# A planner that orders single engine parts by their own data needs, loads in order of use, row sums apart from values, and a second expert weight pack over early memory

## The chip, the cores and the metric

The kernel runs on one core of one Trainium2 chip. The metric is the device time of one execution in microseconds, as the median of several runs. The core has five engines, each with its own instruction queue worked in order: PE (matrix products and transposes, written into PSUM banks), ACT and DVE (element work; they also empty the banks), POOL (small element work), and SP (issues the DMAs). They meet only at semaphores.

## The reference

Four layers, each a cross-attention and a feed-forward block with a gated residual, on x of 2 sequences x 512 tokens x 128 features, and a context of 2 x 77 tokens:

```
x = x + tanh(g_xattn[0]) * L0_xattn(layernorm(x), ctx, ctx, mask)  # 16 heads of 8, masked
x = x + tanh(g_ffn[0])   * L0_ffn(layernorm(x))                    # 128 -> 512 relu -> 128
x = x + tanh(g_xattn[1]) * L1_xattn(layernorm(x), ctx, ctx)        # one key head for 16 query heads
x = x + tanh(g_ffn[1])   * L1_ffn(layernorm(x))                    # shared silu MLP 352 + 16 experts x 64, top 2
x = x + tanh(g_xattn[2]) * L2_xattn(layernorm(x), ctx, ctx)
x = x + tanh(g_ffn[2])   * L2_ffn(layernorm(x))                    # 32 experts x 32, top 1 by argmax
x = x + tanh(g_xattn[3]) * L3_xattn(layernorm(x), ctx)             # 3 iterations of slot attention with a GRU cell
x = x + tanh(g_ffn[3])   * L3_ffn(layernorm(x))                    # int8 product with one 128 x 128 matrix
```

All experts are computed for all tokens, and the router's weights are multiplied in.

## The kernel before

**Tiling.** A "half" is one sequence: 512 tokens, 4 tiles of 128. Everything of a half (x, xn, q, wide and so on) has its own copy, so that the two halves never wait for each other's data. They share the engines, the 8 PSUM banks and the weights. A third stream, "preparation", makes keys and values of all layers, masks and constants of the slot layer.

**The steps of a half.** A layer normalisation is `norm` (DVE statistics, POOL power -0.5) and `norm_end` (DVE writes xn). `turn` transposes xn (PE, ACT). Attention is `query`, four `maxima` (PE scores, DVE row maxima), `max_rows`, three `scores` (PE, then ACT writes four exponentials to `wide`), three `values`, each of which multiplies the exponentials both with a head mask (`heads_of`, the row sums) and with the values (`v_cols`), then `sum_rows` (transpose, DVE reciprocal), `spread` (PE brings the reciprocals back, DVE multiplies) and `project`. `bias` on POOL adds biases to x meanwhile. Layer 1's feed-forward has `gates1` (router), `shared`, `experts`, `weights_turn`, `weigh`, `down_shared`, `down1`, `back`. Layer 2's has `router`, `choice_turn`, `hidden2`, `choose`, `down2`. The slot layer has, three times, `square`, `slots_turn`, `slot_products`, `slot_scores`, `hidden`, `slot_inverse`, four `gru`, `gru_r`, `gru_z`, `gru_end`.

**What sets the order.** The order on each engine is made when the program is built, by `schedule()`. `stream_steps` writes the steps of each stream as a list; one step is a chain over several engines with a duration for each (`pe=0.86, act=0.5`). A step waits for the one before it in its list, but for those marked `on` (the next may follow once their first part has ended) and `side` (nobody in the list waits). Half 1 may not start before `LAG` = 21.937 us. At every turn the part that can start first is put next; small constants shift this rank: `PREFER_STREAM`, `PREFER_ENGINE`, `PER_STEP_LEFT`, and `LATER`, a table with one hand-set shift in tenths of a microsecond for each step of each stream (some 190, 190 and 14 numbers from -82 to 40). `EARLY` and `OPEN` = 3 place the expert steps relative to each other; `OPEN` is how many `hidden2` banks may be open before the first `choose`. `BankTurn` gives every PE result the bank that is free first. Where the planner sees PE idle, after `FILL_FROM` = 20 us, `keep_warm` puts products of `ident16` with `halves` (bf16, 512 columns) into the gap, whose result nobody reads.

**Loads.** SP issues all loads in one row at the start (L642 to L668): x of half 0, ctx_t, attn0, cols, consts, x of half 1, mask, halves, ctx_4, rows, and the later weights. Pack ffn2 lies over the memory of ffn1; SP waits for the last expert products of both halves (`banks.full("y", 3, b)`, L670) and then loads it (L671).

## Time and profile before

| | us |
|---|---|
| median of 3 runs | 359.32 |
| the three runs | 359.07, 359.32, 362.11 |
| the profiled execution | 361.95 |
| its span, first to last instruction | 360.2 |
| PE busy in the span | 328.1 (91%) |
| DVE busy | 225.3 (63%) |
| ACT busy | 136.9 (38%) |
| POOL busy | 47.8 (13%) |

The profiled execution is 2.6 us above the median, and 1.75 us of it lie outside the span. PE's busy time contains the products that `keep_warm` adds. Busy shares are means over a start, a middle and an end that have different limits, so each is read by itself.

### The profile page before, as it was taken

The numbers are of one execution on the slowest core, as the hardware profiler recorded it, in microseconds if no ns is written. First come the engines' busy times: TensorE is split into PE (matmuls) and PEld (weight loads), VectorE is DVE, ScalarE is ACT, GpSimd is POOL, SyncE is SP. The second block draws the span as 40 slices with busy tenths as digits, with TensorE's granted clock in tenths as the row PEclk, the third lists the DMA queues.
The fourth block names the chain that finished last, engine by engine and source line by source line (L and its number), as shares of the span: only waits on it lengthen the run. The fifth ranks groups of instructions, "written<-read, shape, count | busy, mean of one in ns | idle before, by whom it ended". The sixth has DMA issues, their size and how long they took to land.

```text
span 360.2 us, 5043 instructions
## 1 busy us (share of the span) xinstructions
PE 328.1 (91%) x1843; PEld 175.3 (49%) x1843; DVE 225.3 (63%) x635; ACT 136.9 (38%) x287; POOL 47.8 (13%) x73
## 2 busy tenths in 40 slices
PE   0789989998888899999999997899999999999994
PEld 0455453463424543554444434455445677677442
DVE  2596574366628551677766728345353797798995
ACT  1226326331451565225321361711232366646200
POOL 6113112031010100010200020101021311101110
PEclk9999999998989999999999999999999999999998
DMA  7940000000000000000000300000000000000001
GB/s 195 354 198 0 2 0 2 1 0 3 0 2 0 2 0 0 2 0 1 1 2 0 118 11 0 2 0 2 0 0 0 2 1 2 0 2 0 0 14 47
DMA packets 6669, 8.68 MB, mean 24 GB/s; under 512 B 2907, under 2 KB 5493, under 8 KB 6389
## 3 DMA queue, kind: packets, MB, share of 16 engines
q1 hardware_dynamic: 6645, 8.37, 7.0%
q8 instruction: 15, 0.25, 0.3%
q14 instruction: 9, 0.07, 0.1%
HBM read 7.84 MB, written 0.52 MB: 23 GB/s over the span
## 4 chain that ended last, share of the span: by engine, by line
PE 76%; DVE 15%; ACT 6%; issue 1%; DMA 1%; SPq 0%; DVEq 0%; ACTq 0%
PE psum L754 68%; DVE mx L1443 6%; ACT wide L1124 4%; PE psum L838 3%; DVE wide L1610 1%; PE psum L956 1%; PE psum L874 1%; DMA w_attn<-in_attn 1%; PE psum L1052 1%; PE psum L1079 1%; ACT xn_t L1124 1%; PE psum L791 0%; DVE rinv_d L1452 0%; DVE wide L1575 0%; DVE rinv L1449 0%
## 5 line engine op out<-in xcount | busy, mean ns | idle before, releaser
L754 PE MATMUL psum<-xn_t,w_ffn 128*128 128x512 f32 (+1 forms) x136 | 66.6, 608 | 0.8 <-ACT xn_t L1124 0.8
L754 PE MATMUL psum<-wide,w_ffn 128*128 128x512 f32 (+1 forms) x92 | 47.4, 603 | 0.5 <-DVE wide L1535 0.3
L754 PE MATMUL psum<-halves 128*128 128x512 bf16 x178 | 43.9, 379 | 0.2 <-DVE q_lo L1435 0.2
L1443 DVE TENSOR_REDUCE mx<-psum 128x4 f32<-128x308 f32 x96 | 38.7, 471 | 7.3 <-PE psum L754 7.1
L1124 ACT ACTIVATE wide<-psum 128x512 f32<-128x512 f32 x72 | 36.6, 624 | 11.0 <-PE psum L754 10.8
L1124 ACT ACTIVATE q<-psum 128x512 f32<-128x512 f32 (+1 forms) x40 | 23.5, 594 | 44.1 <-PE psum L754 43.8
L754 PEld LDWEIGHTS psum<-xn_t,w_ffn 128*128 128x128 f32 (+1 forms) x136 | 24.9, 190 | 28.8 <-issue 25.9
L698 POOL TENSOR_SCALAR nw<-mv 128x4 f32<-128x4 f32 x16 | 3.6, 227 | 218.7 <-DVE mv L1309 218.7
L754 PEld LDWEIGHTS psum<-halves 128*128 128x128 bf16 x178 | 17.3, 99 | 17.2 <-issue 1.7
L1315 DVE TENSOR_SCALAR xn<-x,mv,nw 128x128 f32<-128x128 f32 x64 | 17.8, 347 | 10.9 <-POOL nw L699 10.7
L754 PE MATMUL psum<-w_attn,q 128*128 128x128 f32 x192 | 23.7, 276 | 0.2 <-DVE q L1459 0.2
L754 PEld LDWEIGHTS psum<-wide,w_ffn 128*128 128x128 f32 (+1 forms) x92 | 16.3, 192 | 15.0 <-issue 8.5
L754 PEld LDWEIGHTS psum<-w_attn,q 128*128 128x128 f32 x192 | 22.5, 192 | 2.0 <-issue 1.1
L1124 ACT ACTIVATE xn_t<-psum 128x512 f32<-128x512 f32 x18 | 11.1, 615 | 30.5 <-PE psum L838 16.5
L1124 ACT ACTIVATE wide<-psum,cols 128x512 f32<-128x512 f32 x12 | 8.2, 687 | 31.2 <-PE psum L754 31.2
L754 PE MATMUL psum<-wide,heads_of 128*32 128x512 f32 x144 | 20.0, 626 | 0.0
L754 PE MATMUL psum<-wide,v_cols 128*32 128x512 f32 x144 | 19.6, 614 | 0.0
L1528 DVE TENSOR_TENSOR wide<-q,psum 128x512 f32<-128x512 f32 x16 | 11.0, 685 | 11.4 <-PE psum L754 9.8
L754 PE MATMUL psum<-wide 78*128 78x386 f32 x48 | 17.8, 496 | 0.2 <-DVE wide L1598 0.2
L699 POOL TENSOR_TENSOR nw<-nw,minus_half 128x4 f32<-128x4 f32 x16 | 16.6, 1036 | 1.3
L1306 DVE BATCH_NORM_STATS2 stats<-x 128x6 f32<-128x128 f32 x64 | 13.9, 280 | 3.9 <-DMA x<-in_x 3.5
L1435 DVE SCALAR_TENSOR_TENSOR q_lo<-psum,cols,q_hi 128x512 fp32r<-128x512 f32 x6 | 4.5, 751 | 18.5 <-ACT q_hi L1180 18.5
(208 smaller groups left out, 492.5 us busy)
## 6 DMA issues: line engine op xcount, KB each, us to landing
w_ffn<-in_ffn SPq DMA_DIRECT2D x1, 2088.5 KB, 12.6
w_ffn<-in_ffn SPq DMA_DIRECT2D x1, 1104.0 KB, 5.0
w_attn<-in_attn SPq DMA_DIRECT2D x1, 640.0 KB, 8.1
w_attn<-in_attn SPq DMA_DIRECT2D x2, 288.0 KB, 5.8
x<-in_x SPq DMA_DIRECT2D x2, 256.0 KB, 3.1
w_ffn<-in_ffn SPq DMA_DIRECT2D x1, 512.0 KB, 6.7
out<-x SPq DMA_DIRECT2D x2, 256.0 KB, 2.3
rows<-in_rows SPq DMA_DIRECT2D x1, 468.0 KB, 6.0
```

Source lines behind the costliest of these rows:

```text
L699: G.tensor_tensor(nw[:, b, 2, :], nw[:, b, 0, :], minus_half[:, :], ALU.pow)\
L754: return nc.tensor.matmul(out_, lhs, rhs, start=start, stop=stop, **kw)
L838: last = nc.tensor.transpose(bk[:, t * P:(t + 1) * P], (y if stage == 7 else xn)[:, b, t, :], ident)
L874: last = nc.tensor.transpose(bk[:, t * P:(t + 1) * P], mx[:, b, t, :], ident)
L956: last = nc.tensor.transpose(bk[:, t * P:(t + 1) * P], tile[:, b, t * P:(t + 1) * P], ident)
L1052: last = nc.tensor.transpose(bk[:, t * P:(t + 1) * P], slots[:, b, t, :], ident)
L1124: A.activation(dst, banks.bank(*name)[0:rows_, 0:cols_], fn, **kw).then_inc(drained["act"], 1)
L1306: last = V.bn_stats(stats[:, b, t, :], x[:, b, t, :])
L1315: last = V.tensor_scalar(xn[:, b, t, :], x[:, b, t, :], mv[:, b, t, 0:1], nw[:, b, 2, t:t + 1], ALU.subtract, ALU.mult)
L1435: V.scalar_tensor_tensor(q_lo[:, b, :], banks.bank("q", layer, b), col(f"bq{layer}"), q_hi[:, b, :].bitcast(F32), ALU.add, ALU.subtract).t ...
L1443: last = V.tensor_reduce(mx[:, b, t, lane_heads(g)], banks.bank("max", layer, b, t, g)[:, 0:GK].rearrange("p (h k) -> p h k", k=CTX), AX.X ...
L1528: V.tensor_tensor(wide[:, b, c, :], act_s[slot][:, b, :], banks.bank("e_u", b, c), ALU.mult)\
```

## The change

1. `schedule()` is replaced. Every step is split into its parts on single engines, and each part names the parts that it reads from (`after`, `then`). A part can be planned once these are planned. `left` is the length of the longest chain of parts that hang on it. The rank is its earliest time, plus `later`, minus 0.1 x `left`. `LAG`, `PREFER_STREAM`, `PREFER_ENGINE`, `PER_STEP_LEFT`, `EARLY` and `OPEN` go. `LATER` now is one number for each stream: 0 for half 0, 2.1 us for half 1, -0.7 us for the preparation. `LOADED` gives the time at which a part's load is taken to have landed.
2. `values` is split into `sums` (row sums) and `values`; each has its own bank and its own exit on ACT. `shared` and `experts` become 11 pairs of `gate` and `up`; `back` at stage 3 is split, with `back_shared` for the shared MLP; `hidden` of the slot layer becomes three.
3. `spread` uses a transpose instead of a product with the identity.
4. Loads: cols, the identity alone, wq of layer 0 and ctx_t go ahead; x of half 1 goes behind ctx_4. `turn` 0 no longer waits for POOL's constants.
5. ffn2 now lies over the masks, attn0 and ffn0 (tile `early`), and its load waits for `y` of stage 1.
6. Eight products on a zeroed tile run on PE before its first step; one memset on DVE makes the tile.

```diff
-LAG = 21.937
-PREFER_STREAM = 0.0, 0.075, -0.739
-PREFER_ENGINE = {"pe": 0.0, "act": 1.11, "dve": 0.291, "pool": 1.091}
-PER_STEP_LEFT = 0.008
-OPEN = 3
+LEAD = {("pe", "turn"): 0.3}
+LEFT = 0.1
+WARM_UP = 8
+LOADED = {("dve", "norm", 0, 0): 3.4, ("pe", "keys_in", 2, 0): 5.0, ("pe", "turn", 0, 0): 4.2, ("pe", "query", 0, 0): 4.8,
+          ("dve", "mask_parts", 2): 6.5, ("pe", "values_in", 2, 0): 9.5, ("dve", "norm", 1, 0): 10.0,
...
         for j in range(NJ):
-            step("values", layer, j, on=j < NJ - 1, pe=1.72, **({"act": 1.0} if j == NJ - 1 else {}),
-                 after=[(PREPARATION, "values_in", layer), (b, "scores", layer, j)])
-        step("sum_rows", layer, pe=0.44, dve=0.92)
-        step("spread", layer, pe=0.88, dve=0.6)
+            evicted = {"act": 0.5} if j == NJ - 1 else {}
+            for phase, made in (("sums", 0), ("values", layer)):
+                step(phase, layer, j, after=[at("act", "scores", layer, j), prepared("dve", "values_in", made)]
+                     + in_order("pe", phase, layer, j), pe=0.86, **evicted)
+        step("sum_rows", layer, after=[at("act", "sums", layer, NJ - 1)], pe=0.44, dve=0.92)
+        step("spread", layer, after=[at("dve", "sum_rows", layer)], then={"dve": [at("act", "values", layer, NJ - 1)]},
+             pe=0.44, dve=0.6)
...
+        for st in waiting:
+            if all(steps[key].end is not None for key in st.after):
+                at = max([steps[key].end for key in st.after], default=0.0) - LEAD.get(st.key[:2], 0.0)
+                at = max(at, free[st.engine], LOADED.get(st.key, 0.0))
...
+                if st.engine == "pe":
+                    at = max(at, banks.deal(units_of(st.phase, st.half, st.args), drained)[1])
+                if at < float("inf"):
+                    rank = at + st.later - LEFT * st.left
...
             load_x(0)
+            sp.dma_start(cols[:, :], a["cols"]).then_inc(loaded["cols"], 16)
+            sp.dma_start(consts[:, 0:P], a["consts"][:, 0:P]).then_inc(loaded["ident"], 16)
+            sp.dma_start(packs["attn0"][:, 0:wq_n], a["attn0"][:, 0:wq_n]).then_inc(loaded["wq0"], 16)
             sp.dma_start(ctx_t[:, :], a["ctx_t"]).then_inc(loaded["ctx_t"], 16)
...
-                sp.wait_ge(*banks.full("y", 3, b))
+                sp.wait_ge(*banks.full("y", 1, b))
             sp.dma_start(packs["ffn2"][:, :], a["ffn2"]).then_inc(loaded["ffn2"], 16)
...
                 for t in range(T):
-                    last = mm(bk[:, t * P:(t + 1) * P], rinv_d[:, b, t, :], ident)
+                    last = nc.tensor.transpose(bk[:, t * P:(t + 1) * P], rinv_d[:, b, t, :], ident)
...
+            def gate(b, k):
+                r = SHC[k][1] if k < SHARED else P
+                if k >= 2:
+                    act.wait_ge(*banks.emptied("up", b, k - 2))
+                empty(act_s[k % 2][0:r, b, :], ACT.Silu, ("gate", b, k), r)
```

## Rows read from the trace of the kernel before

**Rows 1.** The head of the page: span, and busy time of each engine.
```profile
span 360.2 us, 5043 instructions
PE 328.1 (91%) x1843; PEld 175.3 (49%) x1843; DVE 225.3 (63%) x635; ACT 136.9 (38%) x287; POOL 47.8 (13%) x73
```

**Rows 2.** Busy time of each engine by stretch; first column is the stretch.
```profile
core 0: us, PE busy (x) PEld busy (x) DVE busy (x) ACT busy (x) POOL busy (x), PEclk, DMA share, GB/s
0.00:54.00 54.00, 39.91 (x293) 22.82 (x294) 34.79 (x104) 17.05 (x35) 14.56 (x26) 1.00 0.37 125
54.00:288.00 234.00, 221.87 (x1177) 110.45 (x1174) 130.14 (x383) 89.89 (x173) 25.94 (x35) 0.99 0.02 6
288.00:361.00 73.00, 66.28 (x378) 42.07 (x376) 60.39 (x149) 29.96 (x80) 7.31 (x12) 0.98 0.03 8
```

**Rows 3.** Groups by form, PE, the idle products: whole span, then from 288.
```profile
L754 PE MATMUL psum<-halves 128*128 128x512 bf16 x178 | 43.9, 379 | 0.2 <-DVE q_lo L1435 0.2
...
L754 PE MATMUL psum<-halves 128*128 128x512 bf16 x136 | 31.8, 379 | 0.0
```

**Rows 4.** Chain that ended last, first 50 us: start, length, what.
```profile
5.98 1.28 ACT L1128
...
9.07 1.25 DVE minus_max L1361
...
12.56 2.07 PE psum L754 x2
...
17.04 6.27 DVE mx L1443 x16
```

**Rows 5.** Instructions in order of time (start, length, engine), the first layer normalisation and query.
```profile
5.23 1.04 POOL L699 TENSOR_TENSOR nw<-nw,minus_half 128x4 f32<-128x4 f32 x1
...
10.25 1.10 DVE L1315 TENSOR_SCALAR xn<-x,mv,nw 128x128 f32<-128x128 f32 x4
...
14.68 0.69 ACT L1180 ACTIVATE q_hi<-psum,cols 128x512 fp32r<-128x512 f32 x1 [2.16 <-PE psum L754]
```

**Rows 6.** The page's DMA issues: size, us to landing.
```profile
halves<-in_halves SPq DMA_DIRECT2D x1, 384.0 KB, 5.6
```

**Rows 7.** Groups by form, PE: spread, the transposes of maxima, the row sums.
```profile
L754 PE MATMUL psum<-consts,rinv_d 128*128 128x128 f32 x48 | 6.7, 283 | 2.8 <-DVE mx L1443 2.5 <-DVE rinv_d L1452 0.3
...
L874 PE MATMUL psum<-consts,mx 128*128 128x128 f32 x24 | 3.9, 283 | 0.9 <-DVE mx L1443 0.9
...
L754 PE MATMUL psum<-wide,heads_of 128*32 128x512 f32 x144 | 20.0, 626 | 0.0
```

**Rows 8.** DVE in order of time: half 1's maxima ahead of half 0's spread.
```profile
46.47 3.16 DVE L1443 TENSOR_REDUCE mx<-psum 128x4 f32<-128x308 f32 x8
49.56 0.67 DVE L1459 TENSOR_TENSOR q<-q,psum 128x512 f32<-128x512 f32 x1
```

**Rows 9.** DVE in order of time: the shared MLP's way back into x.
```profile
167.81 1.13 DVE L1542 SCALAR_TENSOR_TENSOR x<-psum,route_s,x 128x128 f32<-128x128 f32 x4 [0.20 <-PE psum L956]
```

**Rows 10.** DVE in order of time: hidden, then the inverse, in the slot layer.
```profile
282.35 0.68 DVE L1588 SCALAR_TENSOR_TENSOR wide<-psum,hidden_bias 128x512 f32<-128x512 f32 x1
...
282.95 0.15 DVE L1597 RECIPROCAL nmax<-nmax 77x1 f32<-77x1 f32 x1
```

**Rows 11.** ACT: a group by form, then two of its table loads in time.
```profile
L1124 ACT ACT_TABLE_LOAD x5 | 6.4, 1283 | 1.4 <-PE psum L754 1.3
...
133.26 1.28 ACT L1124 ACT_TABLE_LOAD   x1
...
142.51 1.28 ACT L1124 ACT_TABLE_LOAD   x1 [1.33 <-PE psum L754]
```

**Rows 12.** Two short stretches, columns as in rows 2.
```profile
96.00:102.00 6.00, 4.11 (x56) 2.72 (x60) 3.10 (x13) 4.10 (x9) 2.53 (x3) 0.97 0.00 0
...
102.00:105.00 3.00, 3.00 (x16) 0.41 (x12) 0.00 (x0) 2.48 (x5) 0.00 (x0) 0.50 0.03 5
```

**Rows 13.** PE in order of time: the first transposes of half 0 and of half 1.
```profile
10.73 1.15 PE L838 MATMUL psum<-consts,xn 128*128 128x128 f32 x4 [4.84 <-DVE xn L1315]
...
34.31 0.60 PE L838 MATMUL psum<-consts,xn 128*128 128x128 f32 x4
```

**Rows 14.** Waits of SP's queue: us in total, times, longest.
```profile
SPq L670 <- PE psum L754: 191.2, 1, 191.2
```

More of the change, by code:

```diff
@@ new lines, in __init__, with all_steps, chain, step @@
+    def __init__(self, key, us, after):
+        self.key, self.us, self.after = key, us, after
+        self.engine, self.phase, self.half, self.args = key[0], key[1], key[2], key[3:]
+        self.later, self.left, self.end = 0.0, us, None
+def all_steps():
+    steps = {}
+    def chain(b):
+        def step(phase, *args, after=(), then=None, **takes):
+            previous = list(after)
+            for engine, us in takes.items():
+                key = engine, phase, b, *args
+                steps[key] = Step(key, us, previous + (then or {}).get(engine, []))
+                previous = [key]
+        return step
+    prepare_steps(chain(PREPARATION))
+    for b in range(B):
+        half_steps(b, chain(b))
+    return steps
@@ L162, in attention @@
+        step("max_rows", layer, after=[at("dve", "maxima", layer, T - 1)], pe=0.45, act=0.5)
         for j in range(NJ):
-            step("scores", layer, j, on=True, pe=0.95 if layer else 1.95, act=1.95, after=[(PREPARATION, "masks")])
+            ready = [at("act", "max_rows", layer), at("dve", "query", layer), prepared("pool", "keys_in", layer)]
+            if not layer:
+                ready.append(prepared("act", "masks"))
+            step("scores", layer, j, after=ready + in_order("pe", "scores", layer, j), pe=0.95 if layer else 1.95, act=1.95)
@@ L175, in stream_steps @@
-    step("turn", 1, lead=0.3, pe=0.44, act=0.5)
-    for m in range(C0 + 1):
-        if m < C0:
-            step("hidden0", m, on=True, pe=0.86, **{"act" if m % 2 else "dve": 0.62})
-        if m:
-            down("down0", m - 1, C0, [(b, "hidden0", m - 1)])
-    step("back", 1, pe=0.44, dve=0.65, after=[(b, "bias", 1)])
-    norm(2)
-    attention(2, 1)
-    step("turn", 3, lead=0.3, pe=0.44, act=0.5)
-    step("gates1", on=True, pe=0.8, dve=3.16, act=0.2)
-    for i in range(len(SHC)):
-        step("shared", i, on=True, pe=1.72, act=0.5, dve=0.6)
@@ new lines, in half_steps @@
+    step("slots_back", after=[at("dve", "gru_end", ITERS - 1)], dve=0.65)
+    norm(7, [at("dve", "slots_back")])
+    turn(7)
+    step("quantised", after=[at("dve", "turn", 7), prepared("dve", "slots_in", 4)], pe=0.25, dve=1.83)
+def schedule():
+    steps = all_steps()
+    for b, tenths in LATER.items():
+        for st, later in zip([st for st in steps.values() if st.half == b], tenths):
+            st.later = later / 10
+    followers = {key: [] for key in steps}
+    for st in steps.values():
+        for key in st.after:
+            followers[key].append(st)
+    for st in reversed(list(steps.values())):
+        st.left = st.us + LANDS[st.engine] + max([other.left for other in followers[st.key]], default=0.0)
@@ L281, in schedule @@
[L281 to L294 removed]
+    drained, fillers = {}, {}
@@ L303, in schedule @@
-        free[engine] = at + us
-        st.ends.append(at + us + LANDS[engine])
-        for name, reader in finished_by(st.phase, st.stream, st.args):
-            if reader == engine:
-                drained[name] = st.ends[-1]
-        orders[engine].append((st.phase, st.stream, st.args))
-        if len(st.ends) == len(st.takes):
-            streams[st.stream].remove(st)
-            if not st.side:
-                done_at[st.stream] = max(done_at[st.stream], st.ends[0] - LANDS["pe"] if st.on else st.ends[-1])
+            banks.take(units, drained)
@@ L313, in schedule @@
+        free[st.engine] = at + st.us
+        st.end = at + st.us + LANDS[st.engine]
+        for name, reader in finished_by(st.phase, st.half, st.args):
+            if reader == st.engine:
+                drained[name] = st.end
+        orders[st.engine].append((st.phase, st.half, st.args))
+        waiting.remove(st)
     return orders, banks.dealt, fillers
```

482 lines of the change are left out of this document (236 added, 246 removed), and 43 rows, old and new, of the table LATER.

## The prediction

> **What bounds the kernel now.** I read the page's head first: PE is busy 328.1 of 360.2 us, DVE 225.3, ACT 136.9 [rows 1]. So the question is what PE's time is made of, not whether another engine is full. The groups by form answer it: 178 products of the idle kind, `halves` with `halves`, take 43.9 us of PE's busy time [rows 3]. PE's real work is 328.1 - 43.9 = 284.2 us. The other 76.0 us of the span are PE waiting or idling on purpose. A change of order can only win these 76 us back, and a change of work only moves the 284.
>
> The table by stretch shows where they lie [rows 2]. From 0 to 54 PE is busy 39.9, so 14.1 us are empty. From 54 to 288 it is busy 221.9 of 234: 12.1 us empty. From 288 to the end of the span at 360.2 it is busy 66.3 of 72.2: 5.9 us empty, and 31.8 us of idle products on top [rows 3], so 37.7. What is left of the 43.9 after these 31.8 is 12.1, nearly all of it in the middle, which makes 24 there. The start is 14, the middle 24, the end 38.
>
> The end is the GRU of both halves, a chain over PE, ACT, DVE and POOL. DVE is busy 60.4 of its 72 us [rows 2], 84%. No order removes that work, so from the end's 38 I expect little. The middle is 90% real PE work; half of the end's waiting per microsecond at most can be had there. The start is a plain chain [rows 4]: table load, key parts, first transposes, first query, and only at 17.04 the first row maxima, which then run 6.27 us.
>
> **The change, part by part.**
>
> *Start.* POOL has the standard deviation of half 0 ready at 5.23 + 1.04 = 6.27, but DVE writes xn only at 10.25, because the key parts stand ahead of it in its queue, `minus_max` last, 9.07 to 10.32 [rows 4, 5]. By data needs alone xn can start at about 6.4, ahead of the keys, which need k_t, behind ACT's table load of 1.28 us [rows 4]. From start of xn to the end of q_hi it takes 14.68 + 0.69 - 10.25 = 5.1 us [rows 5], so q_hi is there at 11.5 instead of 15.4, and the first maxima could run at about 17.04 - 15.37 = 1.7 later, 13.2; without the mask transposes, which stand between in PE's queue, at 12. The mask and `halves` must be there too: `halves` lands 5.6 us after its issue [rows 6], and it is issued ahead of x of half 1 now, so they do not bind. That is a lead of 4 to 5 us for half 0. The eight products at the start cover the 2.07 us that the first query took for two passes [rows 4], which are 1.02 us later on in the trace; at most 1 us, within the lead. Not all of a lead reaches the end: what follows is DVE's (34.8 of 54 us busy, maxima of both halves and the preparation). Bounds: 0, if DVE's preparation work only moves behind, and 6. I take 4.
>
> *Later start of x of half 1.* It moves behind seven issues, but half 1's first transposes were at 34.31 [rows 13]. Cost nothing; its cover is over 20 us.
>
> *Spread.* 24 products of two passes, 48 instructions, 6.7 us, become 24 transposes; those of the maxima, also 24 of the same shape, take 3.9 [rows 7]. Saving 2.8, all on PE. Where PE is full it counts whole, and where it is not the chain is shorter by 0.4 each time. Bounds 1.5 and 3.5; I take 3.
>
> *Sums apart from values.* 144 instructions of row sums take 20.0 us, so the six attentions have 3.3 us each, 1.1 for each of three chunks [rows 7]. Before, sums and values alternate, and `sum_rows` starts after ACT has emptied the sums, behind the last values chunk. Now the last values chunk and its exit lie beside `sum_rows` and its reciprocal. That shortens each attention's chain by 1.1 + 0.6 (an exit on ACT) at most, 6 x 1.7 = 10 us over both halves. It only counts where PE has nothing from the other half, and only 24 of 234 us in the middle are like that. There is a second effect of the same kind: half 0's `spread` waits in DVE's queue behind 3.16 us of half 1's maxima [rows 8]; a rank by what is left on the chain puts the longer chain first. Bounds 0 and 8; I take 3.
>
> *Shared MLP back early.* 1.13 us of DVE [rows 9] and four transposes leave the chain behind the last expert product, twice. Covered by the other half's work mostly. Bounds 0 and 3; I take 1.
>
> *Hidden in three.* In the slot layer the reciprocal that the four GRU products wait for starts at 282.95, behind `hidden`'s 0.68 at 282.35 [rows 10]. Now it waits for its own exponentials only. Up to 0.7 us on DVE and as much on PE for each of three iterations of half 1, which ends last: bounds 0 and 4; I take 2.
>
> *ffn2 over early memory.* SP waited 191.2 us for this load's release [rows 14]. It will issue it after stage 1 of both halves instead. Behind it in SP's queue are only the stores at the end. Routers no longer need the other half's experts done; before, the load was not late for anyone, so I cost it at nothing. Without it the planner could not move router work ahead, which matters only if the halves drift further apart.
>
> *Table loads.* Here the change costs. ACT holds one set of functions: between the loads at 133.26 and 142.51 it ran half 1's exponentials, and silus of half 0 on either side [rows 11]. Each change is 1.28 us, and there are five at this line. Neither planner has a term for it. The old order has the silus of a half in near-closed runs; the new one places every `gate` and every `scores` by its own time, and half 0's 11 gates meet half 1's three groups of exponentials, then the reverse. Up to two more changes for each group, 12 in all, 15 us of ACT, none of them planned. ACT has room (137 of 360 us), but the part behind a load is late by 1.28, and PE's queue is in order. Bounds 0 and 15; I take 2, four more loads at half their price, since gates can run ahead by only two slots of `act_s` and so wait for DVE in between anyhow.
> The Trainium skill, page "ScalarE: Activation LUTs", section "What ACT_TABLE_LOAD costs", speaks against the change here: a switch is 1283 ns plus a drain of about 1380, so 2.66 us. The row agrees on the 1283; by 2.66 those four would cost 4 us more at half price, and 2 more than in my sum.
>
> Sum: -4 -3 -3 -1 -2 +2 = -11 us. On the profiled execution's own 361.95 that is 351.0 (span 349.2); on the median 359.32 it is 348.3. I predict 348.
>
> What I leave at nothing is the loss of some 390 hand-set shifts. They bought whatever the old planner's coarse lists could not say; no row shows how much.
>
> **The rivals.**
>
> *Tables.* All 12 extra changes come and none is hidden: 15 us instead of 2, so 359.3 - 13 + 15 = 361. To end more than 1% slower it needs 17 us, 13 exposed loads, which the gates with their eight expert and three shared pieces can reach if they alternate with the other half's `gates1` exponentials too: 16 loads, 20 us, 367. For it: a greedy rank sees no price in alternating. Against it: ACT is idle 62% of the span.
>
> *Halves in step.* Half 1 no longer waits 21.9 us; it may start once x has landed, against a handicap of 2.1 us in the rank. The lag was 34.31 - 10.73 = 23.6 us [rows 13], and with it one half's maxima, 6.27 us of DVE with hardly a microsecond of PE in layers 1 and 2 [rows 4], lie under the other half's products. If the lag falls under two such stretches, 13 us, PE has nothing to put there: some 4.7 us for each of six, so 28 at worst, 359 - 11 + 28 = 376. It decides from four uncovered stretches on. Against it: 0.1 x `left` and 2.1 balance at a difference of 21 us of chain, so half 0 is preferred until it is that far ahead; a later stage repairs what the start spoils.
>
> *No net gain.* The start's lead is spent in DVE's queue and the rest lies in time that PE filled with idle products: -2 to +2, 357 to 361.
>
> *More than forecast.* Each term at its far bound without table cost: 6 + 3.5 + 8 + 3 + 4 = 24.5, so 335. The free order may also fill the middle's 24 us. For it: 22 product parts of `gate` and `up` in each half, which now may go into any gap.
>
> *Clock.* After 96 to 102, with PE busy 4.11 of 6 us, the granted clock was 0.50 for the 3 us that follow, the 1.2 GHz level, with PE busy all through [rows 12]. Such a stretch costs 1.5 us. If each of six spreads brought one, 9 us, and the time would be 357.
> By the skill's page "TensorE: Matmul & The Clock Gate", "Part 4: PE-mode transpose", transposes do not count as PE activity, which would make this likelier; no run here shows it yet.
>
> **How the numbers follow.** Within 1% is about what a measurement of this kernel can tell from no change: 355.7 to 362.9. The forecast's own case, a gain of 4 to 23 us by the terms above, has 0.50. More than forecast, under 336, has 0.10. No net gain, with the clock case and tables at their first price in it, has 0.18. Tables beyond 13 exposed loads 0.11, halves in step 0.11. So faster 0.60, same 0.18, slower 0.22. The range leaves out 0.07 below 334 and 0.13 above 366, by the two slower rivals' dear ends.
>
> **What would show it.** Start: first maxima of half 0 at 12 to 13 us, and xn at about 6.4. Spread: 24 instructions of about 3.9 us together. Sums: `heads_of` products in runs of four with `sum_rows` before the last `v_cols`. End: reciprocal of the inverse ahead of `hidden`. Table loads: count them; seven to eleven is my case, twenty the rival's. Lag: the first transposes of half 1 against half 0, and again at each stage. Loss in the middle would show as empty PE between 54 and 288 above 12 us. I am wrong if PE's empty and idle time stays near 76, or if it grows in the middle by more than the start gains.

## The result

| | median us | executions | ratio to before |
|---|---|---|---|
| before | 359.7 | 4, 359.07 to 362.11 | |
| after | 371.55 | 4, 369.81 to 372.34 | 1.0295, 95% interval 1.025 to 1.034 |

The change made the kernel 3% slower, where 3% faster was forecast. The forecast's 348 and its range 334 to 366 both missed. The quotient of the two medians is 1.033; the kernel before came out lower here than in its 60 later executions, whose median is 360.96, and by that it is 1.029. A ratio leaves out executions in a slower state, more than 1.5% above the fastest of the same kernel (three in all, one each of before_transpose, after_cold and after_search), so it is not always the quotient of the medians shown.

The head of the page and the table by stretch of the changed kernel (columns as in [rows 2]) answer [rows 1, 2]:

```profile
span 370.0 us, 5017 instructions
...
PE 335.4 (91%) x1817; PEld 172.8 (47%) x1817; DVE 224.3 (61%) x636; ACT 143.3 (39%) x291; POOL 48.3 (13%) x73
...
0.00:54.00 54.00, 42.22 (x282) 22.03 (x282) 32.81 (x101) 17.67 (x35) 15.26 (x27) 0.94 0.37 125
54.00:288.00 234.00, 221.67 (x1146) 106.32 (x1143) 128.16 (x374) 94.08 (x169) 22.56 (x29) 0.96 0.02 6
288.00:370.00 82.00, 71.49 (x394) 44.42 (x392) 63.31 (x162) 31.55 (x88) 10.49 (x17) 0.98 0.03 7
```

The last three figures of a stretch begin with the granted clock: 0.94, 0.96 and 0.98, where [rows 2] has 1.00, 0.99 and 0.98. PE is busy longer although it was given less to do, and from 288 on there are 82 us in place of 72.

The groups by form of PE answer [rows 3, 7]: the idle products, the new products at the start, the spread and the row sums.

```profile
L806 PE MATMUL psum<-halves 128*128 128x512 bf16 x168 | 42.5, 392 | 0.3 <-DVE mx L1506 0.3
L806 PE MATMUL psum<-wide 128*128 128x512 bf16 x8 | 3.5, 625 | 1.2 <-DVE wide L1716 1.2
L986 PE MATMUL psum<-consts,rinv_d 128*128 128x128 f32 x24 | 3.8, 280 | 0.7 <-DVE rinv_d L1515 0.7
L806 PE MATMUL psum<-wide,heads_of 128*32 128x512 f32 x144 | 19.1, 602 | 0.9 <-issue 0.6 <-ACT wide L1193 0.3
```

So PE waits or idles 370.0 - 335.4 + 42.5 + 3.5 = 80.6 us, against 76.0 before, and its real work is 335.4 - 42.5 - 3.5 = 289.4 us, against 284.2. The span grew by 9.8: 4.6 of waiting and 5.2 of work. The work should have shrunk by 2.9, since the spread's 6.7 us [rows 7] became 3.8. So there are some 8 us of work more than the instructions explain, since these are the same ones in another order.

**Where the clock fell.** Five stretches of the changed kernel ran at 0.50, the 1.2 GHz level: 7.9 to 14.8, 79.6 to 83.0, 110.3 to 120.6, 223.0 to 226.4, and the last few us. The kernel before had two of 3.4 us, from 84.6 and from 101.7 [rows 12], and the last few us. What the engines did in all of these together, the changed kernel first, then the kernel before:

```profile
sum 27.53, PE 21.11 PEld 13.39 DVE 18.93 ACT 5.45 POOL 3.92; mean PE 4.22 PEld 2.68 DVE 3.79 ACT 1.09 POOL 0.78
sum 9.33, PE 6.82 PEld 1.81 DVE 2.29 ACT 2.56 POOL 0.33; mean PE 2.27 PEld 0.60 DVE 0.77 ACT 0.85 POOL 0.11
```

If everything that PE did there took twice its time, the low clock cost 10.6 us in one and 3.4 in the other, so some 7 us of the difference; that is an estimate, and it has the idle products in these stretches in it. It is not all of the 8 us with certainty: in the table below, xn_first_one_table and before_transpose both ran at .990 with the same real instructions, and the new order's has 286.2 us of work for 282.7. A part of PE's busy time comes with the order and not with the clock; why is not shown.

The longest stretch of the changed kernel in short windows, columns as in [rows 2]:

```profile
105.00:108.00 3.00, 1.22 (x10) 0.64 (x10) 2.93 (x9) 0.39 (x1) 0.00 (x0) 1.00 0.00 0
108.00:111.00 3.00, 1.28 (x7) 0.68 (x7) 2.97 (x14) 0.00 (x0) 1.26 (x2) 0.89 0.00 0
111.00:120.00 9.00, 9.00 (x24) 5.09 (x24) 6.82 (x23) 2.48 (x3) 0.00 (x0) 0.50 0.00 0
```

Ahead of it PE is busy 2.5 of 6 us while DVE is busy 5.9. Then PE is busy for all of 9 us, at half its rate. What DVE and PE did there, in order of time (start, length, engine, line, out and in):

```profile
105.04 0.75 DVE L1409 SCALAR_TENSOR_TENSOR x<-psum,gain,x 128x512 f32<-128x512 f32 x1 [1.31 <-PE psum L806]
...
105.82 1.64 DVE L1506 TENSOR_REDUCE mx<-psum 128x4 f32<-128x308 f32 x4
...
107.22 0.41 PE L806 MATMUL psum<-keys_hi,q_hi 32*128 32x308 f32 x4 [1.42 <-DVE mx L1506]
107.37 0.86 DVE L1369 BATCH_NORM_STATS2 stats<-x 128x6 f32<-128x128 f32 x4
...
108.57 1.60 DVE L1506 TENSOR_REDUCE mx<-psum 128x4 f32<-128x308 f32 x4
...
109.16 0.41 PE L806 MATMUL psum<-keys_hi,q_hi 32*128 32x308 f32 x4 [1.53 <-DVE mx L1506]
...
110.12 1.11 DVE L1378 TENSOR_SCALAR xn<-x,mv,nw 128x128 f32<-128x128 f32 x4
...
115.06 7.29 PE L806 MATMUL psum<-xn_t,w_ffn 128*128 128x512 f32 x10
```

Half 0's way from `project` to xn and half 1's maxima of layer 1 want DVE at the same time and take turns. PE has 0.41 us of scores for each 1.6 us of maxima, and nothing of half 0. What comes next are half 0's gates, plain full products, ten of them in 7.29 us. The weight loads between such products show the pace across the end of the stretch:

```profile
119.49 0.34 PEld L806 LDWEIGHTS psum<-xn_t,w_ffn 128*128 128x128 f32 x1 [0.52 <-issue]
120.35 0.31 PEld L806 LDWEIGHTS psum<-xn_t,w_ffn 128*128 128x128 f32 x1 [0.52 <-issue]
120.90 0.16 PEld L806 LDWEIGHTS psum<-xn_t,w_ffn 128*96 128x96 f32 x1 [0.24 <-issue]
121.33 0.16 PEld L806 LDWEIGHTS psum<-xn_t,w_ffn 128*96 128x96 f32 x1 [0.27 <-issue]
```

One product each 0.85 us inside it, one each 0.43 behind it.

### The profile page after: what moved, and what is told of

Same layout as the page of the kernel before. It is cut to its first block, busy times and chain, and to the rows that moved or that the text cites. A ratio compares the mean times of both kernels' runs of the same rounds, so it can differ in the third digit from the quotient of the medians.

```text
span 370.0 us, 5017 instructions
## 1 busy us (share of the span) xinstructions
PE 335.4 (91%) x1817; PEld 172.8 (47%) x1817; DVE 224.3 (61%) x636; ACT 143.3 (39%) x291; POOL 48.3 (13%) x73
## 4 chain that ended last, share of the span: by engine, by line
PE 66%; DVE 20%; ACT 7%; issue 3%; DMA 1%; SPq 0%; POOL 0%; POOLq 0%; DVEq 0%; ACTq 0%
PE psum L806 59%; DVE mx L1506 5%; PE psum L892 2%; ACT wide L1193 2%; DVE xn L1378 1%; ACT q L1193 1%; PE psum L1010 1%; DVE stats L1369 1%; DVE wide L1663 1%; DVE wide L1670 1%; PE psum L978 1%; DVE wide L1669 1%; ACT L1193 1%; DVE nmax L1634 1%; PE psum L930 1%
## 5 line engine op out<-in xcount | busy, mean ns | idle before, releaser
L806 PE MATMUL psum<-xn_t,w_ffn 128*128 128x512 f32 (+1 forms) x88 | 46.6, 640 | 0.0
L806 PE MATMUL psum<-halves 128*128 128x512 bf16 x168 | 42.5, 392 | 0.3 <-DVE mx L1506 0.3
L1193 ACT ACTIVATE q<-psum 128x512 f32<-128x512 f32 (+1 forms) x40 | 23.6, 596 | 46.5 <-PE psum L806 44.0
L1506 DVE TENSOR_REDUCE mx<-psum 128x4 f32<-128x308 f32 x96 | 38.7, 469 | 3.8 <-PE psum L806 3.7
L806 PE MATMUL psum<-xn_t,early 128*128 128x512 f32 x52 | 27.9, 625 | 0.1
L1581 DVE TENSOR_TENSOR wide<-q,psum 128x512 f32<-128x512 f32 (+1 forms) x22 | 14.7, 684 | 21.7 <-PE psum L806 18.8
L806 PEld LDWEIGHTS psum<-xn_t,w_ffn 128*128 128x128 f32 (+1 forms) x88 | 16.2, 200 | 19.9 <-issue 15.8
L806 PE MATMUL psum<-wide,early 128*128 128x512 f32 x48 | 24.8, 605 | 0.0
L1409 DVE SCALAR_TENSOR_TENSOR x<-psum,gain,x 128x512 f32<-128x512 f32 x12 | 9.0, 750 | 25.3 <-PE psum L1010 16.1
L806 PE MATMUL psum<-wide 78*128 78x386 f32 (+1 forms) x56 | 21.4, 516 | 3.2 <-DVE wide L1651 2.0
L1193 ACT ACTIVATE xn_t<-psum 128x512 f32<-128x512 f32 x18 | 10.7, 597 | 29.2 <-PE psum L892 22.8
L806 PE MATMUL psum<-wide,w_ffn 128*128 128x512 f32 (+1 forms) x44 | 21.9, 597 | 0.1
L806 PE MATMUL psum<-keys_hi,q_hi 32*128 32x308 f32 x96 | 10.4, 417 | 11.3 <-DVE mx L1506 8.4
```

The lines of the kernel that those rows point to most:

```text
L806: return nc.tensor.matmul(out_, lhs, rhs, start=start, stop=stop, **kw)
L1193: A.activation(dst, banks.bank(*name)[0:rows_, 0:cols_], fn, **kw).then_inc(drained["act"], 1)
L1409: V.scalar_tensor_tensor(flat(x[:, b, :, :]), banks.bank("out", stage, b), gain[:, g:g + 1], flat(x[:, b, :, :]), ALU.mult, ALU.add).then_ ...
L1506: last = V.tensor_reduce(mx[:, b, t, lane_heads(g)], banks.bank("max", layer, b, t, g)[:, 0:GK].rearrange("p (h k) -> p h k", k=CTX), AX.X ...
L1581: V.tensor_tensor(wide[0:r, b, at_, :], act_s[k % 2][0:r, b, :], banks.bank("up", b, k)[0:r, :], ALU.mult)\
```

## The experiments

All ratios are to the kernel before, executed on the same chip in the same stretch of time; brackets are 95% intervals. The interval of one ratio is about 0.004 to 0.007 wide on either side, 1.5 to 2.5 us, and for the difference of two ratios it is 0.007 to 0.009, so differences under 0.007 are not told apart. "Waiting" is span less PE's busy time plus all idle products, "work" the rest of PE's busy time, both of the profiled execution, which is not always near the median: for plan_tables, after_lag_5 and xn_first_one_table it is 2.5 to 3.2 us below it, for after_cold 4 above. Before and before_one_table do the same on PE and differ by 2.1 us in each, so nothing smaller is read from them. Part of this is in the records: in before_one_table, after_one_table, after_xn_first and before_transpose 17 or 18 products are missing from the profile (1826 products for 1843 weight loads in the first), most of them idle ones; in before_one_table this moves some 2 us from waiting to work.

| run | median us | ratio | waiting | work | granted clock |
|---|---|---|---|---|---|
| before | 359.7 | | 76.0 | 284.2 | .987 |
| after | 371.55 | 1.0295 | 80.6 | 289.4 | .963 |
| after_one_table | 368.87 | 1.0209 | 74.8 | 292.5 | .962 |
| before_one_table | 361.15 | 1.0010 | 73.9 | 286.4 | .987 |
| after_xn_first | 366.66 | 1.0158 | 73.6 | 290.9 | .981 |
| xn_first_one_table | 363.68 | 1.0056 | 72.5 | 286.2 | .990 |
| xn_first_filled | 368.30 | 1.0200 | 78.2 | 287.4 | .979 |
| before_transpose | 361.54 | 1.0014 | 76.5 | 282.7 | .990 |
| after_matmul_spread | 371.18 | 1.0299 | 80.2 | 288.7 | .979 |
| after_cold | 371.04 | 1.0243 | 80.3 | 293.3 | .964 |
| after_lag_5 | 376.70 | 1.0448 | 80.8 | 291.6 | .940 |
| plan_tables | 370.28 | 1.0254 | 75.7 | 289.5 | .981 |
| before_xn_first | 356.86 | 0.9886 | 72.5 | 283.6 | .991 |
| before_no_shifts | 386.01 | 1.0667 | 98.3 | 286.6 | .970 |
| after_search | 359.83 | 0.9973 | 67.4 | 290.0 | .981 |

### Table loads

ACT has eleven table loads in the changed kernel, seven before:

```profile
L1193 ACT ACT_TABLE_LOAD x8 | 10.3, 1283 | 0.2
L1275 ACT ACT_TABLE_LOAD x2 | 2.6, 1283 | 0.0
L1197 ACT ACT_TABLE_LOAD x1 | 1.3, 1283 | 5.7 <-PE psum L806 5.7
```

Seven of them lie between 112 and 140 us. Silu is made Tanh in both kernels, so that one set of functions serves the whole kernel; the values of the shared and expert parts then differ from the reference's.

```diff
-                empty(act_s[k % 2][0:r, b, :], ACT.Silu, ("gate", b, k), r)
+                empty(act_s[k % 2][0:r, b, :], ACT.Tanh, ("gate", b, k), r)
```

> The changed kernel with tanh in place of silu in the gate step, so that one table of ACT holds every function (the expert and shared MLP values are not the reference's). It removes 10 of 11 table loads of 1.28 us. Theory tables (the unplanned loads between 112 and 140 cost the gain): 8 us or more faster than the changed kernel's 371.6, about 361 to 363. Theory clock and theory lag: ACT's loads are mostly hidden, at most 3 us faster, 368 to 371.

Measured: 368.87 us, ratio 1.0209 [1.0153, 1.0266]. The ten loads cost 1.0295 - 1.0209 = 0.9%, 3.1 us of their 12.8, just beyond the noise of such a difference.

> The kernel before with the same exchange of silu for tanh (values of the expert and shared MLP are not the reference's); it removes 6 of 7 loads. Control for the run above: if tables tell the two kernels apart, this gains clearly less than the other, 0 to 3 us, 357 to 360. If both gain the same, the extra loads are not what makes the change slower.

Measured: 1.0010 [0.9977, 1.0043]. In the kernel before, six loads, 7.7 us of ACT, cost nothing: every `turn` starts 0.08 to 0.13 us later than it did. So what a load costs depends on the order that it falls in. The Trainium skill ("ScalarE: Activation LUTs", "What ACT_TABLE_LOAD costs") gives a drain of some 1380 ns on top of the 1283; by that figure ten loads would be 26.6 us of ACT, an estimate. The traces agree on the 1283, and neither sum is seen at the end of the kernel.

### The start

xn stands where it stood, 10.87 for 10.25 [rows 5], and the first transposes are later, 12.34 for 10.73 [rows 13]. DVE and PE of the changed kernel in order of time, the first transposes last:

```profile
7.48 0.24 DVE L1419 CAST k_hi<-k_t 128x154 fp32r<-128x154 f32 x1 [1.52 <-ACT k_t L1197]
...
8.70 1.33 DVE L1424 TENSOR_SCALAR minus_max<-lane_mask 128x308 fp32r<-128x308 f32 x1
...
10.19 0.31 DVE L1432 TENSOR_SCALAR early<-early 128x308 f32<-128x308 int32 x1
...
10.55 1.99 PE L846 MATMUL psum<-consts,early 128*77 128x128 f32 x8 [4.95 <-DVE early L1432]
...
10.87 1.10 DVE L1378 TENSOR_SCALAR xn<-x,mv,nw 128x128 f32<-128x128 f32 x4
...
12.34 1.06 PE L892 MATMUL psum<-consts,xn 128*128 128x128 f32 x4
```

The new planner still puts the keys and now the mask parts ahead of xn. Its own plan ends the copy of k_t at 5.80 and half 0's deviations at 5.98, so the keys go first, and at 7.60 the masks. On the chip k_t is ready only at 6.98 + 0.39 = 7.37, behind ACT's table load of 1.28 us at 5.69, which no plan knows. DVE waits 1.52 us for it, up to 7.48, and from 6.45 on xn's inputs are at hand.

```diff
+def ahead(engine, step, of_):
+    ORDERS[engine].remove(step)
+    ORDERS[engine].insert(ORDERS[engine].index(of_), step)
+
+
+ahead("dve", ("norm_end", 0, (0,)), ("keys_in", PREPARATION, (0,)))
+for engine in ("pe", "act"):
+    for phase in ("turn", "query"):
+        ahead(engine, (phase, 0, (0,)), ("masks", PREPARATION, ()))
```

> The changed kernel with half 0's first norm_end ahead of the key parts on DVE, and its turn and query ahead of the mask transposes on PE and ACT: what the prediction took the new order to be. Theory start (the lead that was forecast never came, because DVE's order puts xn behind keys and masks): xn at 6.5 in place of 10.9, first maxima 3 to 4 us earlier, and 2 to 4 us less in all, 367.5 to 369.5. Theory clock: the lead is taken back by the same hole of both halves near 105 and the half clock behind it, 371 or so.

Measured: 366.66 us, ratio 1.0158 [1.0095, 1.0221]. xn is written at 6.36, the first transposes run at 6.85, and of the lead of 5.5 us the last turn keeps 5.5 (357.85 for 363.32). The stretch at 0.50 from 7.6 us goes, and two short ones with it; the 10.2 us one stays and begins at 105.

Both edits together:

> The kernel of after_xn_first with tanh in place of silu in the gate step (values of the expert and shared MLP are not the reference's), so that one table serves all. If the start order and the tables are separate costs that add, 366.7 - 2.7 = 364.0. If the tables' cost only shows through the clock or the start, 366 to 367.

Measured: 363.68 us, ratio 1.0056 [1.0025, 1.0087]. Start and tables add up: 2.4% of 3.0%. What is left is 2 us, with an interval of 1 us on either side.

The same move, alone, in the kernel before (the line for DVE only; its PE order has the turn first already):

> The kernel before with one move: VectorE normalizes half 0 ahead of the copies of the keys' inputs. In the kernel before xn is written at 10.25 us and the first transposes start at 10.73; moved the same way in the changed kernel, xn stood at 6.36 and the transposes at 6.85, and 4.9 us of 371.55 went. If the start is worth the same wherever it is made, the ratio here is about 0.99 (3 to 4 us less, 356 to 357 us). If what counts is the order behind the start, whose slack swallows an earlier first turn, the turns end earlier only for half 0 and the time stays at 359 to 361 us. If the earlier start comes with a stretch at the lower granted clock at 7 to 14 us, as in the changed kernel, it is lost there: then the mean clock is under .987.

Measured: 356.86 us, ratio 0.9886 [0.9843, 0.9929], 4.1 us faster than before. This is faster than both kernels.

```profile
6.38 1.11 DVE L1317 TENSOR_SCALAR xn<-x,mv,nw 128x128 f32<-128x128 f32 x4 [1.55 <-POOL nw L701]
...
6.87 1.15 PE L840 MATMUL psum<-consts,xn 128*128 128x128 f32 x4 [0.26 <-DVE xn L1317]
```

The lead of 3.9 us at xn arrives at the end nearly whole: the span is 356.1 for 360.2, and at an equal mean clock of .997 the time is 355.6 and 356.1 for 359.2, 3.4 us less.

The eight products ahead of the first transposes:

```diff
-WARM_UP = 8
+WARM_UP = 0
```

> The changed kernel with no idle products ahead of the first transposes (8 of them, 1.2 to 4.7 us, go). If they raise the clock for the work of the start, it should be later here: the 6.8 us stretch at the lower clock from 7.6 us stays or grows and the time rises by 0 to 2 us. If they only move the low stretch, the time stays at 370 to 372 us and the granted clock of the first 54 us stays near .94.

Measured: 371.04 us, ratio 1.0243 [1.0168, 1.0318], its executions from 367.06 to 375.36, the slowest being the profiled one. The stretch at 0.50 in the first 54 us is gone (granted clock there 1.00 for 0.94), and PE waits where the products were. No gain and no loss can be told from this; with so wide a spread it stays open. The four executions do follow their clock: .986 went with 367.1 us, .981 with 369.7, .972 with 372.4 and .964 with 375.4.

### The spread

```diff
-                    last = mm(bk[:, t * P:(t + 1) * P], rinv_d[:, b, t, :], ident)
+                    last = nc.tensor.transpose(bk[:, t * P:(t + 1) * P], rinv_d[:, b, t, :], ident)
```

This edit alone, in the kernel before:

> The kernel before with one part of the change alone: spread by transposes. By PE's work 2.8 us less, 356.5 to 357.5. If transposes leave the clock low more often: no gain, or slower than 359.5, with more of the span at a granted clock of 0.50.

```profile
L928 PE MATMUL psum<-consts,rinv_d 128*128 128x128 f32 x24 | 3.8, 281 | 2.8 <-DVE mx L1443 2.5 <-DVE rinv_d L1452 0.3
```

Measured: 1.0014 [0.9980, 1.0048]. The spread on PE takes 3.8 us for 6.7 [rows 7], 2.9 less, as forecast, and the time is the same: PE still waits 2.8 us in front of it. And the other way round, products in the changed kernel:

> The changed kernel with the spread of the inverses made by products again, 6.7 us for a turn's in place of 3.8. By the forecast's term this costs 24 instructions' difference, 2.9 us: 374 us. By the run of the kernel before with transposes (ratio 1.0014) it costs nothing: 371 us. If transposes don't keep the clock up as products do, the mean granted clock rises from .963 and the time falls to 366 to 369 us.

Measured: 371.18 us, ratio 1.0299 [1.0236, 1.0362]. The time is again the same. The clock moved both times the way that the Trainium skill has it ("TensorE: Matmul & The Clock Gate", "Part 4: PE-mode transpose": a transpose doesn't count as busy time of PE in the way a product does): executions of before_transpose had .971 to .990 where before had .985 to .997, and after_matmul_spread had .970 to .989 where the four of after had .963 to .972. In the kernel before the clock doesn't account for the missing gain: at .990 before_transpose took 360.5 to 361.7, and before, at .991 and .992 on the same chip, 360.2 to 361.1.

In the changed kernel it stays open. With products the longest low stretch is 3.4 us in place of 10.2, though the hole ahead of it is there (columns as in [rows 2]):

```profile
108.00:111.00 3.00, 0.41 (x4) 0.22 (x4) 2.97 (x14) 0.28 (x1) 0.21 (x1) 1.00 0.00 0
111.00:114.00 3.00, 2.59 (x10) 1.25 (x11) 3.00 (x11) 0.15 (x1) 1.05 (x2) 0.55 0.00 0
```

PE is busy 0.41 of 3 us, even less than in the changed kernel, and the time is not shorter for the higher clock. Either the products' 2.9 us and what the clock gave back cancel, or the clock is worth less here than in the kernel before; the noise of these two ratios, some 2.8 us, doesn't tell.

### The long hole at 103 us

If the half clock of 110 to 120 us comes from PE having little to do while DVE has too much, idle products in that place should hold it up. Twelve are put among half 1's maxima that the kernel numbers 2, in after_xn_first:

```diff
-                bks = [start_unit("max", layer, b, t, g) for g in range(LANES)]
+                bks = []
+                for g in range(LANES):
+                    bks.append(start_unit("max", layer, b, t, g))
+                    if (b, layer) == (1, 2) and t:
+                        keep_warm(bks[g], 1)
```

> The kernel of after_xn_first (366.7 us) with 12 idle products of 0.22 us, one ahead of each of half 1's layer-2 maxima groups for tiles 1 to 3, where PE waits for DVE to empty banks just ahead of the 10.2 us at the 1.2 GHz level. They add 2.6 us of PE work to a hole and touch nothing else. Theory clock (PE's sparse work in that hole lets the clock fall, and the 10.2 us of full PE work behind it run at half rate): the low stretch is gone or shorter, up to 5 us less, 361.5 to 364.5. Theory that the clock only goes along: no change or up to 1 us more, 366.5 to 368.

Measured: 368.30 us, ratio 1.0200 [1.0133, 1.0267], not told apart from 1.0158 without the products. The low stretch is still there in the profiled execution:

```profile
102.00:105.00 3.00, 0.75 (x8) 0.54 (x8) 2.97 (x14) 0.00 (x0) 0.67 (x2) 0.88 0.00 0
105.00:108.00 3.00, 2.88 (x12) 1.16 (x8) 3.00 (x10) 0.67 (x2) 0.59 (x1) 0.50 0.00 0
```

But the experiment missed its place. The kernel counts the attentions from 0, and the maxima ahead of the low stretch are those of number 1 (the reference's layer 1); number 2 comes some 110 us later. The idle products by stretch (PE busy and count first, then weight loads), first without the twelve, then with them:

```profile
92.00:112.00 20.00, 2.48 (x5) 0.80 (x6) 0.83 0.01 2
212.00:226.00 14.00, 2.01 (x7) 0.99 (x9) 1.00 0.00 1
```

```profile
92.00:112.00 20.00, 2.69 (x6) 0.80 (x6) 0.81 0.00 1
212.00:226.00 14.00, 5.54 (x20) 1.97 (x20) 1.00 0.00 1
```

Around the hole there are six in both; the added ones lie after 212 us. So this run says nothing on whether work put into the hole keeps the clock up, and that test is still to be made. Its single executions (365.07 us with a mean clock of .993, 367.41 with .979, 369.2 and 369.3 with .975) show only that the clock differs from one execution to the next, 4 us apart.

### The lag between the halves

The halves' shift is 2.1 us in the rank. With 0.5 it is this:

```diff
-    1: (21, 21, 21, 21, 21, 21, 21, 21, 21, 21, 21, 21, 21, 21, 21, 21, 21, 21, 21, 21, 21, 21, 21, 21, 21, 21, 21, 21,
...
+LATER = {0: (0,) * 400, 1: (5,) * 400, 2: (-7,) * 60}
```

> The changed kernel with half 1's handicap in the rank at 0.5 us in place of 2.1, so that both halves run about 8 us apart instead of 25 to 45, and DVE-bound maxima of both halves fall together. Rival halves in step: clearly slower than 371.6, 378 to 395, with more empty PE between 54 and 288. Theory that the changed kernel's large lag (half 1 alone at the end) is what costs: faster, 360 to 368, with the end shorter.

Measured: 376.70 us, ratio 1.0448 [1.0384, 1.0513]. The first transposes of the two halves (PE, in order of time), and the middle stretch (columns as in [rows 2]):

```profile
12.46 1.06 PE L863 MATMUL psum<-consts,xn 128*128 128x128 f32 x4
17.83 0.60 PE L863 MATMUL psum<-consts,xn 128*128 128x128 f32 x4
...
54.00:288.00 234.00, 212.48 (x1066) 103.69 (x1064) 124.30 (x358) 82.64 (x145) 26.04 (x32) 0.92 0.02 6
```

The lag is 5.4 us, PE is busy 212.5 us of the middle where after has 221.7, and the clock is 0.92, with stretches of 20.5 and 13.7 us at 0.50. Halves in step are dear, as the rival said. The changed kernel itself is not in step: its lag is 22.3 us at the start (12.34 and 34.59), against 23.6 [rows 13]. From stage 3, the feed-forward of layer 1, on it is the other way: half 0's turn of stage 3 runs at 110.53 and half 1's at 164.16, 53.6 us apart, where before has 121.05 and 156.81, 35.8. At the end half 1 comes 25.6 us behind half 0, before 11.4. For all that time at the end there is only one half's chain to fill PE.

### The planner told of the loads

```diff
+TABLE_LOAD = 1.28
+TABLE_OF = {"gate": "silu", **dict.fromkeys(("scores", "gates1", "slot_scores", "gru_r", "gru_z", "gru_end", "out_bias"), "exp")}
...
+                if switches(st, table):
+                    at += TABLE_LOAD
```

Two start times are set as well: ACT's copy of k_t not before 6.9, the mask parts not before 8.0.

> The changed kernel's planner told of two things it left out: 1.28 us for each change between silu and the exp set on ACT, and that k_t comes at 6.9 us behind the first table load and the mask at 8.0, so that half 0's xn goes first. No other shift. Theory (the planner's blindness costs the 11 us): loads fall from 11 to 9, start 4 us earlier, 360 to 365. Theory that the plain order without tuned shifts is the loss: still 366 or more.

Measured: 370.28 us, ratio 1.0254 [1.0199, 1.0308], with nine loads. It has the early xn of after_xn_first (1.0158) and fewer loads, and is not better than that. A planner that knows more but still picks greedily made another order, not a better one. That is the outcome named for the second theory, an order without tuned shifts: start and tables are causes, but not the root.

### The shifts

What the forecast "left at nothing" was the loss of the hand-set shifts. The planner's own end times say what they hold. Counted from each plan's first transposes, since the old plan starts at 0 and the new one knows the loads, and beside them the same stretch of the chip:

| | plan | chip | chip less plan |
|---|---|---|---|
| before | 340.7 - 3.7 = 337.0 | 360.2 - 10.7 = 349.5 | 12.5 |
| before, shifts at 0 | 362.2 - 3.7 = 358.5 | 384.9 - 10.9 = 374.0 | 15.5 |
| after | 338.3 - 9.5 = 328.8 | 370.0 - 12.3 = 357.7 | 28.9 |
| plan_tables | 343.1 - 7.0 = 336.1 | 365.2 - 6.9 = 358.3 | 22.2 |
| after_search | 337.1 - 7.0 = 330.1 | 357.4 - 6.9 = 350.5 | 20.4 |

By its plan the changed kernel is 8.2 us shorter than the kernel before (328.8 for 337.0), and on the chip it is 8.2 longer: its plan leaves out 16 us more. So the plan alone would have misled as well. The figures of plan_tables are those of an execution 3 us below its median.

The shifts of the old planner at zero (the table has 382 entries, 275 of them not zero):

```diff
...
-    2: (6, -33, 6, 1, -4, 18, -19, -15, -5, 25, -4, -3, -1, 0),
+    0: (0,) * 184,
+    1: (0,) * 184,
+    2: (0,) * 14,
```

> The kernel before with all 382 hand-set shifts of its table at zero; planner, steps and instructions stay. The forecast left their loss at nothing. The old planner's own end time for this order is 362.2 us against 340.7 with the shifts, and 338.3 is what the new planner promises with none: so the shifts hold 21.5 us of plan, and the changed kernel had to win that back before it could gain. If the plan is right on the chip, the time here is 376 to 384 us, and the new planner alone is worth about 10 us against an untuned old one, though it is slower than the tuned one. If the shifts are worth nothing, as the forecast had it, the time is 359 to 362 us. If shifts were fitted to the chip and not to the plan, the loss is over 25 us.

Measured: 386.01 us, ratio 1.0667 [1.0625, 1.0710]: 24.1 us. The head of its page and its idle products:

```profile
span 384.9 us, 5128 instructions
...
PE 342.0 (89%) x1887; PEld 184.4 (48%) x1887; DVE 224.5 (58%) x635; ACT 134.7 (35%) x285; POOL 48.0 (12%) x73
...
L742 PE MATMUL psum<-halves 128*128 128x512 bf16 x222 | 55.4, 387 | 0.5 <-issue 0.5
```

Nearly all of it is waiting: 384.9 - 342.0 + 55.4 = 98.3, against 76.0; and it has two table loads fewer than before. Now the reverse: the new planner with shifts of its own. 210 of the 785 entries of its table are set by a random search that makes the plan short and its stretches with little PE work few; the planner knows the loads as in plan_tables.

> The changed kernel with shifts of its own: 210 of the 785 entries of its table are set by a random search over the plan, and the planner is told of ACT's table loads of 1.28 us and of the later start of the keys. Planned end 337.1 us with 8 changes of function set in it; the same planner without the search promised 343.1 and ran at 370.3. If the loss against the kernel before is an order without shifts, the 6.0 us of plan come back on the chip with a few more by fewer low-clock stretches: 360 to 365 us. If plan and chip part because half 0 runs far ahead (planned lag at stage 3 is 46.7 us, 34.3 in the kernel before), it stays at 366 to 371. If it is all clock, the time follows the mean granted clock: 360 at .99, 368 at .965.

Measured: 359.83 us, ratio 0.9973 [0.9943, 1.0004], as fast as before.

```profile
span 357.4 us, 4963 instructions
...
PE 329.4 (92%) x1791; PEld 167.2 (47%) x1791; DVE 223.4 (63%) x636; ACT 140.8 (39%) x289; POOL 48.9 (14%) x73
...
L795 PE MATMUL psum<-halves 128*128 128x512 bf16 x142 | 35.8, 390 | 0.0
```

Waiting is 67.4 us (28.0 empty, 35.8 and 3.6 of idle products), 8.3 less than plan_tables, whose planner it shares and which runs at 1.0254. So the searched shifts are worth 2.8%, 10.1 us, to the new planner, and the tuned ones 6.7% to the old. Its low stretches hold 10.2 us of PE's time besides the last few us, against 6.8 in the kernel before. Its lag at stage 3 is 52.1 us on the chip (104.50 and 156.55), nearly that of the changed kernel: a long lag by itself does not make it slow.

## Why the prediction was wrong

**The step that failed** is the one-sentence step after the sum: "What I leave at nothing is the loss of some 390 hand-set shifts". No row showed their price, and I put 0 where a bound was needed. The run before_no_shifts gives 24.1 us for them. Against an old planner without shifts the new one is 1.0667 - 1.0295 = 3.7% faster, 13 us, and the 24.1 us of shifts that went with the change are more. The 13 us do not confirm the terms of my sum, of which start and spread did not come (below); they are the worth of the new rule and the new steps together. I used the trace of a tuned order as if it were that of a planner's rule.

The lost shifts are not the whole of it: the new plan promised to make up for them (328.8 for 337.0) and the chip did not follow. Table loads and low stretches are in that gap of 16 us; the rest of it is open, and so is the worth of each single part of the change but the spread.

**What the changed order pays on the chip**: (a) xn stays behind keys and masks, 4.9 us, but the kernel before pays 4.1 for the same, so this is hardly a part of the difference; (b) gates and exponentials alternate, 3.1 us; (c) DVE is asked for maxima and for a norm at once, PE has a hole and then runs at half clock. That the one makes the other is argued from their order in time, not shown. These overlap: moving xn also took three of the low stretches away. The clock as a whole is some 7 us by the low stretches. By the kernel before, whose time follows its clock (below), .987 to .963 is 0.024 x 321 = 7.7 us, an estimate that reaches beyond the .985 to .997 it rests on.

By the prediction's own steps:

- *Start, -4.* The size was right: moved in the kernel before, xn gave 4.1 us, and in the changed one 4.9. Whether the change moves it was wrong. I wrote that "by data needs alone xn can start at about 6.4", and didn't work the rank out: keys ready at 5.80 against 5.98, with the table load not in the plan. The first thing I said would show it, xn at 6.4, stood at 10.87.
- *Spread, -3.* The 2.9 us less on PE were there (the 3 that I took is already more than the 2.8 that I worked out), the gain was not: 1.0014 in one kernel, 1.0299 for 1.0295 in the other. "Where PE is full it counts whole" failed; the spread stands beside a wait (2.8 us, mostly for `mx`), which is still there with the shorter spread.
- *Sums, -3.* The mechanism came. In order of time, half 0 of layer 1:

```profile
98.65 1.06 PE L806 MATMUL psum<-wide,heads_of 128*32 128x512 f32 x8 [0.30 <-ACT wide L1193]
...
99.53 1.04 PE L806 MATMUL psum<-wide,v_cols 128*32 128x512 f32 x8
...
99.78 0.60 ACT L1193 ACTIVATE xn_t<-psum 128x512 f32<-128x512 f32 x1 [1.19 <-PE psum L806]
...
100.52 0.64 PE L978 MATMUL psum<-consts,xn_t 128*128 128x128 f32 x4
```

  The sums leave their bank at 99.78 while the values are multiplied, and `sum_rows` starts at 100.52, 0.8 us after the last row sum, where the kernel before took 1.8 (109.58 to 111.37). It stands behind the last `v_cols` product here, and ahead of it in two of the six attentions only. Its own worth was not measured apart from the order; that stays open.
- *Hidden in three, -2.* The reciprocal now starts at 298.05, ahead of `hidden` at 298.55. It was 282.95 behind 282.35 [rows 10]. It is ahead in all six iterations. The end's waiting is 38.7 us, for 37.7, so no gain is seen there. Shown is that the step happened, not what it is worth.
- *Table loads, +2.* Eleven loads, four more, as taken; the ten that could be removed cost 3.1 us, and the six of the kernel before nothing. The size was right within the noise. The rival with thirteen exposed loads did not come. The sentence beside it that prices four loads at 2.66 us is wrong in its own sums: at half price that is 5.3 us, 3 more than the term.
- *ffn2, 0.* Issued at 91.75 instead of behind stage 3; no wait on it is seen.
- *Clock.* The rival had 9 us and the sign, from the spreads' transposes. The size was near the 7 estimated. Whether the transposes have a share in it is open: without them the clock was higher, .970 to .989, and the time the same. It had no chance of its own, but 0.18 shared with no net gain, and no time beyond 357.
- *No net gain.* The nearest by mechanism: waiting stayed near 76, which was my own mark for being wrong, and it grew to 80.6.

The range was too narrow on the slow side: beyond 366 I had only the dear ends of tables (367) and of halves in step (376). A loss in a term without a row should have been there.

## What to carry to other kernels

When a planner's rule is replaced, run the old rule without its tuned constants, or at least plan it (here 362.2 for 340.7 by plan): only against that is the new rule measured, and the constants' price (here 24 us, more than every term of the change) belongs in the sum. Don't take the new plan's end for the chip's; the gap between plan and chip was 12.5 us for the old planner and 28.9 for the new. Look up where the new rule puts each step that you price, and add to its plan what it doesn't know, a table load on the chain above all. Here the start, a plain chain, paid almost in full: one step moved ahead in one queue gave 4.1 us, more than the whole rewrite with a searched table of shifts. And when an experiment adds instructions to a place, look in its trace whether they stand there.

## What was not expected of the hardware

The kernel before, in the 60 executions that went with the runs, takes a time that its mean granted clock tells (four of the clocks that occur):

| mean clock | executions | mean us |
|---|---|---|
| .997 | 8 | 359.22 |
| .992 | 15 | 360.58 |
| .987 | 13 | 362.04 |
| .985 | 5 | 363.34 |

Over all 60 that is 3.2 us for each 0.01. By these clocks the same program has more time at the 1.2 GHz level in one execution than in the next, so a difference of 1% between two kernels needs many executions, or a look at both clocks. Also new: the six table loads of the kernel before, 7.7 us of ACT, cost nothing that 10 executions without them show.
